# TensorE's projections, transposes and ffn products placed behind the value phase of their step in a relu-attention block

## The reference

```
xn  = layernorm(x)
q, k, v = split(xn @ w_qkv)                     # per head: 8 + 8 + 8 columns
w   = relu(q k^T / sqrt(8));  w = w / (sum(w) + 1e-6)
y   = xn + (w v) @ w_out + b_out
x1  = x + layernorm(y) * gamma + beta
x2  = x1 + sqrt(real^2 + imag^2),  real = layernorm(x1) @ cos(theta + theta_noise)
                                   imag = layernorm(x1) @ sin(phi + phi_noise)
```

## Time and profile before

| what | us |
|---|---|
| median of 3 runs (421.67, 421.72, 548.05) | 421.72 |
| the profiled execution | 422.16 |
| its span, first to last instruction | 420.4 |
| PE busy | 412.1 (98%) |
| ACT busy | 341.1 (81%) |
| DVE busy | 331.6 (79%) |
| TensorE clock granted | 1.0 of full speed |

### The profile page before, as it was taken

One profiled execution on the slowest core, in us unless ns is written; L12 is line 12 of the kernel. 1 busy time (PEld: TensorE's weight loads), 2 busy tenths in 40 slices (PEclk: granted clock), 3 DMA queues, 4 the chain that ended last, 5 costly groups with the idle time before them and its releaser, 6 DMA issues.

```text
span 420.4 us, 8994 instructions
## 1 busy us (share of the span) xinstructions
PE 412.1 (98%) x3263; PEld 120.0 (29%) x3263; DVE 331.6 (79%) x654; ACT 341.1 (81%) x611; POOL 49.4 (12%) x57
## 2 busy tenths in 40 slices
PE   8899999999999999999999999999999999999995
PEld 6333222222222222222222322222222322222234
DVE  5877778888688897777778898777778798777856
ACT  3879888888788888888888888788887888888864
POOL 2004000099101000000401000000100100000111
PEclk9999999999999999999999999999999999999999
DMA  5117841010021100001011100101012000000200
GB/s 168 31 51 147 162 114 51 2 27 25 4 75 46 51 2 21 33 0 52 27 53 55 27 27 8 43 2 52 27 50 58 2 27 1 27 2 27 68 2 25
DMA packets 11741, 17.54 MB, mean 42 GB/s; under 512 B 3684, under 2 KB 5364, under 8 KB 11316
## 3 DMA queue, kind: packets, MB, share of 16 engines
q1 hardware_dynamic: 11556, 16.84, 15.0%
q10 hardware_dynamic: 144, 0.13, 0.1%
HBM read 3.99 MB, written 5.11 MB: 22 GB/s over the span
## 4 chain that ended last, share of the span: by engine, by line
PE 97%; DVE 2%; ACT 1%; issue 0%; POOL 0%; POOLq 0%; DVEq 0%
PE pv L1154 61%; PE sc L1119 27%; PE pv L1212 2%; PE pv L1054 1%; PE pv L1074 1%; PE pv L1066 1%; PE pv L1045 1%; PE pv L1180 1%; PE pv L1161 0%; PE pv L1034 0%; PE sc L1212 0%; PE sc L1081 0%; DVE x L969 0%; PE sc L1161 0%; PE sc L1267 0%
## 5 line engine op out<-in xcount | busy, mean ns | idle before, releaser
L1154 PE MATMUL pv<-w_buf,v_sb 128*32 128x512 f32 x2048 | 272.3, 604 | 0.0
L781 DVE TENSOR_SCALAR w_buf<-sc 128x512 f32<-128x512 f32 x256 | 176.9, 691 | 68.9 <-PE sc L1119 59.2
L603 ACT ACTIVATE w_buf<-sc 128x512 f32<-128x512 f32 x256 | 153.2, 598 | 62.8 <-PE sc L1119 61.5
L609 ACT ACTIVATE w_buf<-sc 128x512 f32<-128x512 f32 (+1 forms) x254 | 182.5, 719 | 0.0
L1119 PE MATMUL sc<-q_rep,k_rep 32*128 32x512 f32 x1024 | 133.2, 494 | 1.0 <-DVE w_buf L781 0.9
L786 DVE TENSOR_SCALAR w_buf<-sc 128x512 f32<-128x512 f32 x182 | 125.0, 687 | 0.0
L1119 PEld LDWEIGHTS sc<-q_rep,k_rep 32*128 32x128 f32 x1024 | 52.0, 181 | 215.0 <-ACT w_buf L603 176.5
L1154 PEld LDWEIGHTS pv<-w_buf,v_sb 128*32 128x32 f32 x2048 | 40.4, 108 | 66.5 <-ACT w_buf L609 35.4
L494 POOL TENSOR_TENSOR oT<-o_raw,o_scale 128x512 f32<-128x512 f32 (+1 forms) x4 | 5.1, 1281 | 88.4 <-issue 60.8
L510 POOL TENSOR_TENSOR mag<-sq 128x256 f32<-128x256 f32 x6 | 4.4, 731 | 77.5 <-ACT sq L649 77.5
L500 POOL TENSOR_TENSOR x<-x,mv 128x512 f32<-128x512 f32 (+1 forms) x5 | 4.3, 870 | 68.2 <-DVE x L883 55.7
(11 more groups left out here) (132 smaller groups left out, 152.3 us busy)
## 6 DMA issues: line engine op xcount, KB each, us to landing
pv_dram<-pv_sb SPq DMA_DIRECT2D x15, 256.0 KB, 2.0
q_rep<-q_hi SPq DMA_DIRECT2D x30, 64.0 KB, 2.1
q_rep<-q_lo SPq DMA_DIRECT2D x30, 64.0 KB, 2.1
k_rep<-k_hi SPq DMA_DIRECT2D x6, 256.0 KB, 4.1
k_rep<-k_lo SPq DMA_DIRECT2D x6, 256.0 KB, 5.4
x_sb<-x_dram SPq DMA_DIRECT2D x3, 256.0 KB, 3.9
o_raw<-pv_dram SPq DMA_DIRECT2D x3, 256.0 KB
o_scale<-inverse_dram SPq DMA_DIRECT2D x3, 256.0 KB
```

The lines of the kernel that those rows point to most:

```text
L603: nc.scalar.activation(w_buf[:, s % W_STEPS, 0, :], early[:, 0, :], ACT.Relu).then_inc(relu[0], 2 if none else 1)
L609: nc.scalar.activation(w_buf[:, s % W_STEPS, 2:2 + n, :], late[:, 0:n, :], ACT.Relu).then_inc(relu[0], 1)
L781: nc.vector.tensor_scalar(w_buf[:, s % W_STEPS, 1, :], early[:, 1, :], 0.0, None, ALU.max).then_inc(relu[1], 2 if both else 1)
L1154: last = nc.tensor.matmul(bank[32 * i:32 * i + 32, :], v_sb[:, k, HPG * g + i, :], w_buf[:, s % W_STEPS, i, :], start=(k == 0), stop=(k == ...
```

## The change

In the loop of TensorE's program (run_pass, L1222) the call of value_step(c, s - LAG) is moved ahead of the hooks. In each step that has a side product PE's order was scores, side product, values, and is now scores, values, side product. Nothing is added or removed, no wait is changed, and the other engines' programs are the same. transpose_x(2) stands in step 1 of pass 0, where there is no value step, and does not move. 24 side products do: 8 in the first group of pass 0, three project_q, ffn_means, and four in each of passes 1 to 3.

```diff
@@ -1230,11 +1230,11 @@
                                 project_k(1)
                             continue
                         g, k = divmod(s - 1, NT)
+                        if s >= LAG:
+                            value_step(c, s - LAG)
                         for at, hook in hooks:
                             if at == (g, k):
                                 hook()
-                        if s >= LAG:
-                            value_step(c, s - LAG)
```

## The result

The changed kernel takes 425.26 us (median of 5 runs, 424.24 to 425.45) against 421.93 us for the kernel before, measured beside it: ratio 1.0076, 95% interval 1.0064 to 1.0088. Measured again in a second group of runs it is 425.21 us, ratio 1.0085 (1.0071 to 1.0099). The change costs 3.2 to 3.6 us, 0.8%, which is under the 2% by which a clear difference was defined and well outside the interval around no change.

What follows compares the result with a forecast made beforehand. PE was taken to set the time, through its own work and its waits for ACT's and DVE's relus. Terms 2.0 + 1.0 + 0.3 = 3.3 us gave 425.5, or 425.0 for the median; 80% range 422.8 to 427.8.

Steps and rivals of the forecast that it cites:

- PE's own work: PE's switches between scores, values and products: reordering them costs 0, bounds -2.6 to +2.6 us over 24 products.
- not slower: Rival: a product behind the values starts sooner on PE, saving 2.6 us, 419 to 421 us in all; chance 0.06.
- The hooks' own waits: First group of pass 0: products waiting for a bank's reader move one value phase later, wait stays 0.13; no cost.
- project_q, 3 x 0.66: Behind project_q(1) to (3), DVE's late q_lo delays its relu: stall 0.73 instead of 0.07, 2.0 us in all.
- project_v(2) and (3), 2 x 0.5: ACT's read of each delays its first relu and stalls the next scores by 0.5, 1.0 us in all.
- project_out, 3 x 0.11: DVE's residual read delays its relu to 0.72 behind the scores' start; three stalls of 0.11, 0.3 us.
- The covered six: project_v(1), project_k(2), (3), (0), project_q(0), transpose_x(3): late relus hidden by the next step's product; 0, some 3 us if uncovered.
- the squares: Six ffn products: ACT's square leaves its relu at 0.60 behind the scores' start, under 0.81; no stall.
- the products read a step later: transpose_x1 and ffn_means: their readers come a step later with 1.4 us of room; no cost.
- DMAs: SP's copies of k and q for the first group start 1 us later; counted 0, at most 1 us.
- No change: Rival: idle ACT and DVE absorb the late reads, time stays 421.7 us; chance 0.10.
- Much slower: Rival: every moved product pays what project_q does, 24 x 0.66 = 15.8 us, giving 437 us; chance 0.04.

Runs made afterwards that it cites:

- f1: The kernel before with only six ffn products, three transpose_x1 and ffn_means moved behind the values: 421.75 us, ratio 1.0008.
- e4: The kernel before with 16 side products behind the values; project_q(1) to (3), project_v(2), (3) and the three project_out stay ahead: 422.93 us, ratio 1.0029.
- f2: The kernel before with only the eight side products of pass 0's first group moved behind the values: 422.43 us, ratio 1.0027.
- e5: The changed kernel with project_v(3) and its reader one step earlier, directly behind project_v(2)'s step: 424.83 us, ratio 1.0076 to the kernel before.
- e6: The changed kernel with project_v(2) and (3) ahead of the values again and DVE's q_lo and residual reads one step later: 423.28 us, ratio 1.0034 to before.
- e7: e6 with times_gamma and first_residual also split into two tiles in each of two steps, ACT taking both late heads: 422.37 us, ratio 1.0018 to before.

## Why the prediction was right

The forecast was 425.0 us, and 425.26 was measured; the sum of its terms was 3.3 us, and the steps of the trace give 3.40. Term by term:

- *PE's own work, 0 (bounds -2.6 to +2.6).* Held. The values last 0.99 to the product and the product 1.06 to the scores, and f1 moves ten products and changes no interval by over 0.03. The rival "not slower", a cheaper switch out of the values, falls with it.
- *The hooks' own waits, unchanged.* Held in the change, as the steps of the first group show. Its reason, that a product, its readers and the next product all come one value phase later, is also its condition: e4 broke the pair and paid 1.0 us.
- *project_q, 3 x 0.66.* Measured 0.65, 0.65, 0.66. The relu was to start at T' + 1.34 and starts at T' + 1.33.
- *project_v(2) and (3), 2 x 0.5.* Measured 0.49 twice; ACT's relu at T' + 1.27 for the 1.29 forecast. The limit of 0.81 for ACT had been read from a single row, behind a table load, and carried over.
- *project_out, 3 x 0.11.* The one term that was off in size: +0.21 or +0.22, of which 0.06 comes back two steps later, 0.15 net. The step that failed is "relu at T' + 0.72". I had taken the 0.61 between q_lo and the next relu for the residual as well; behind the residual, which DVE waits for itself, it is 0.73. In total 0.1 us.
- *The covered six, the squares, the products read a step later: 0.* Held (f1, f2), and e5 shows the cover at work on a product that had none.
- *DMAs, 0.* Held: no interval at the start of a group differs by over 0.03.
- *No change.* This rival rested on idle time averaged over the span, and on the rule of the Trainium skill ("Perfetto Trace Analysis", Identifying the Most-Contended Engine) that performance is improved at the engine with the highest occupancy. Here PE has 98%, no instruction of PE's was added, DVE and ACT are at 78% and 80%, and the kernel is 0.8% slower. The page says which engine to optimize first; that a change which leaves its work alone is free was my conclusion from it, and that is what failed. PE does set the time, but the time was lost at the moments when it waits for one of the others.
- *Much slower.* Behind each of the eight products that cost something only one interval grew, that from the torn scores to the next; a stall gives both engines its length back.

The range, 422.8 to 427.8, was wider than needed: over half of its width came from PE's switch, for which the earlier trace rows already had a measured 0.53. The terms named for it (2.2 to 4.4 us, and 1.3 either way) give 422.6 to 427.4 over 421.7, so its bounds are a little off.

## What to carry to other kernels

In a software pipeline the place of an extra product is set less by the engine that makes it than by the one that reads it: put the product where its reader's queue still has a gap ahead of the next instruction that someone waits for. Measure that gap from one plain step and one late one (here 0.07 us on DVE, 0.27 on ACT, while both idle for a fifth of the time), and price each late read as its excess over the gap, unless the next step has work of its own to cover it. And move neighbours that share a buffer together, since one of a pair alone can turn a hidden release into a wait.

## What was not expected of the hardware

- The start of the program takes two or more lengths with the same instructions. The first scores start at 10.6 us in the profile of before and at 9.5 in that of the change, and at 9.5 to 10.6 in those of the experiments. The row of PE that shows it is the product that centres the weights, 1.49 us before and 0.81 after, while both windows from 4 to 12 us show a granted clock of 1.00. The transposes behind it (L1034, four records) are longer as well, 1.04 against 0.60:

```profile
5.52 1.49 PE L1081 MATMUL sc<-wqkv_sb,x1T 128*128 128x384 f32 x2
```

```profile
5.22 0.81 PE L1081 MATMUL sc<-wqkv_sb,x1T 128*128 128x384 f32 x2
```

  In the two profiles of the change the first scores start at 9.5 and 10.5, and the executions took 424.37 and 425.36. Most likely this is also what spreads a kernel's other runs over some 1.1 us (the change: 424.24 and 424.37, then 425.26 to 425.45), as much as the smaller effects studied here. Its cause stays open.
- Three times DVE began a relu 0.4 us later than its scores allowed, with nothing ahead of it in its queue: in step 57 of pass 0 in both e6 and e7 (0.98 behind the scores, after 1.65 us of idle), and in step 14 of pass 3 in e7 (0.97, after 1.67). The length of the idle does not explain it: without the delay it would have been 1.21 and 1.24, and relus behind 1.20 to 1.36 us of idle, in these kernels and the others, start at 0.53 to 0.62. That step 57 shows it in both kernels speaks for something of that place in the program. Nothing was tried to find the cause.
- Each of ACT's two table loads within the passes costs this kernel 0.37 us of span, not its 1.28 us. The slack of 0.27 takes a part, and in that step DVE takes both late heads (DVE_BOTH_LATE), which spares ACT a relu of 0.59.
